# Attention scores of two heads side by side in the two row halves of TensorE, in three groups over two banks

## What is computed

```
B, S = 2, 512      # x is redrawn with this shape
H, KVH, HD = 32, 8, 64
q = apply_rope((xn @ Wq.T) as (b, H, s, HD))
k = apply_rope((xn @ Wk.T) as (b, KVH, s, HD));  v = (xn @ Wv.T) as (b, KVH, s, HD)
k, v repeated over the 4 heads of a group
logits = einsum('bhqd,bhkd->bhqk', q, k) * HD ** -0.5, masked causally
attn = softmax(logits);  out = einsum('bhqk,bhkd->bhqd', attn, v)
s = out.reshape(b, s, H * HD) @ Wo.T
```

## Time and profile before

| | |
|---|---|
| median of 3 runs | 783.19 us (781.56 to 783.24) |
| profiled execution: time, span | 780.78 us, 779.0 us |
| mean granted TensorE clock | 0.968 |
| PE (TensorE matmul) busy | 706.5 us, 91% |
| DVE (VectorE) busy | 477.7 us, 61% |
| ACT (ScalarE) busy | 417.9 us, 54% |
| POOL (GpSimd) busy | 399.3 us, 51% |

### The profile page before, as it was taken

One profiled execution on the slowest core, in us unless ns is written; L12 is line 12 of the kernel. 1 busy time (PEld: TensorE's weight loads), 2 busy tenths in 40 slices (PEclk: granted clock), 3 DMA queues, 4 the chain that ended last, 5 costly groups with the idle time before them and its releaser, 6 DMA issues.

```text
span 779.0 us, 13360 instructions
## 1 busy us (share of the span) xinstructions
PE 706.5 (91%) x4536; PEld 618.6 (79%) x4536; DVE 477.7 (61%) x1023; ACT 417.9 (54%) x1043; POOL 399.3 (51%) x451
## 2 busy tenths in 40 slices
PE   2999999999999991388889999999999999999995
PEld 2887989989989981266678888888888888888874
DVE  7582644423323445485566787777877778777764
ACT  4446244233233234236467776677766777667663
POOL 1412442332332220326777776787767877677460
PEclk9899999999999996599899999999999999999999
DMA  5075877778787505235224323322233222232001
GB/s 187 28 253 186 280 251 249 237 253 254 248 254 250 171 15 155 41 116 147 82 69 117 67 62 69 89 69 64 65 69 89 71 58 67 58 89 56 1 1 54
DMA packets 101859, 96.21 MB, mean 124 GB/s; under 512 B 50592, under 2 KB 72032, under 8 KB 101664
## 3 DMA queue, kind: packets, MB, share of 16 engines
q1 hardware_dynamic: 99584, 89.33, 39.6%
q0 software_dynamic: 2208, 6.03, 2.2%
HBM read 69.24 MB, written 9.31 MB: 101 GB/s over the span
## 4 chain that ended last, share of the span: by engine, by line
PE 64%; DVE 10%; POOL 9%; ACT 8%; issue 6%; SPq 1%; POOLq 1%; DMA 1%; DVEq 0%; ACTq 0%
PE bank L1631 15%; PE bank L1491 8%; PE bank L1665 8%; PE bank L1492 8%; PE bank L1493 8%; PE bank L1487 6%; POOL prob L1449 5%; ACT prob L1264 3%; PE bank L1752 3%; DVE nmax L1010 2%; PE bank L1753 2%; POOL q_lo L1461 2%; ACT kv_hi L1271 2%; DVE o_lo L1023 1%; POOL wq_lo L1429 1%
## 5 line engine op out<-in xcount | busy, mean ns | idle before, releaser
L1449 POOL TENSOR_TENSOR prob<-prob,rinv 128x128 f32<-128x128 f32 (+3 forms) x256 | 177.6, 724 | 102.1 <-DVE rinv L1015 102.1
L1264 ACT ACTIVATE prob<-bank,nmax 128x512 f32<-128x512 f32 (+3 forms) x256 | 133.2, 528 | 45.4 <-DVE nmax L1010 43.9
L1019 DVE TENSOR_TENSOR kv_lo<-bank,kv_hi 128x512 fp32r<-128x512 f32 x160 | 110.0, 687 | 52.7 <-ACT kv_hi L1271 51.8
L1271 ACT ACTIVATE kv_hi<-bank 128x512 fp32r<-128x512 f32 x160 | 96.3, 602 | 78.7 <-PE bank L1487 78.6
L1631 PEld LDWEIGHTS bank<-xgT,wm 128*128 128x128 f32 x920 | 108.1, 192 | 5.3 <-issue 3.8
L1631 PE MATMUL bank<-xgT,wm 128*128 128x128 f32 x920 | 110.3, 275 | 0.5 <-ACT xgT L1173 0.5
L1487 PE MATMUL bank<-cst,prob 128*128 128x128 f32 x640 | 97.8, 276 | 3.0 <-POOL prob L1449 1.2
L1010 DVE TENSOR_REDUCE nmax<-bank 128x1 f32<-128x512 f32 (+2 forms) x192 | 91.1, 502 | 10.8 <-PE bank L1755 10.2
L1491 PE MATMUL bank<-kv_hi,v_lo 128*128 128x128 f32 (+3 forms) x256 | 93.2, 364 | 0.3 <-DVE kv_lo L1019 0.3
L1752 PE MATMUL bank<-kT,qT 128*128 128x512 f32 (+3 forms) x256 | 81.6, 324 | 11.2 <-ACT prob L1264 7.2
L912 DVE TENSOR_TENSOR hE<-sil,bank 128x512 f32<-128x512 f32 x23 | 15.8, 688 | 111.0 <-PE bank L1631 80.5
(11 more groups left out here) (301 smaller groups left out, 1479.0 us busy)
## 6 DMA issues: line engine op xcount, KB each, us to landing
wm<-in_w_moe SPq DMA_DIRECT2D x23, 1280.0 KB
wm<-in_w_moe SPq DMA_DIRECT2D x23, 640.0 KB, 5.7
qT<-q_hi SPq DMA_DIRECT2D x124, 64.0 KB, 2.0
qT<-q_lo SPq DMA_DIRECT2D x124, 64.0 KB, 2.0
k_exp<-k_rows SPq DMA_DIRECT2D x56, 64.0 KB, 2.0
wtl<-in_w_moe_tail SPq DMA_DIRECT2D x46, 64.0 KB
gy<-y_rows SPq DMA_DIRECT2D x8, 256.0 KB, 4.8
wq_raw<-in_w_qkv SPq DMA_DIRECT2D x32, 64.0 KB, 2.5
```

What stands on the lines that cost most here:

```text
L1019: TT(p_lo[:, b_, :], bank[2 + b_ % 2][:, :], p_hi[:, b_, :].bitcast(F32), ALU.subtract).then_inc(plo_done, 1)
L1264: ins = actv(prob[:, i % 2, h, POFF[j]:POFF[j] + (j + 1) * P], bk[:, at:at + (j + 1) * P], ACT.Exp, bias=nmax[:, i % 2, h, j:j + 1], accum ...
L1271: actv(p_hi[:, b_, :], bank[2 + b_ % 2][:, :], ACT.Copy).then_inc(phi_done, 1)
L1449: ins = GT(seg, seg, rinv[:, i % 2, k, j:j + 1].to_broadcast([P, (j + 1) * P]), ALU.mult)
```

## The change

- `SCORES` has three groups per pair instead of five. A group holds the same blocks j for both heads: block 3; blocks 2 and 0; block 1. Head 0 goes to bank 0, head 1 to bank 1, so each group fills both banks.
- `qT` and `kT` keep their size; a head's high and low part of q now lie in two slots on the same 64 rows, head 0 on rows 0 to 63 and head 1 on rows 64 to 127. A score is the sum of three products over 64 rows (low q with high k, high q with low k, high with high); the product of the two low parts is left out. The products of the two heads alternate, placed at array row 0 and row 64.
- The mask is one product per head: 6 a pair instead of 5, 1024 columns instead of 1280.
- S and E stand at steps 0, 1.7 and 3.4 of a pair instead of 0 to 4; N of the two heads at 4.6 and 6 instead of 3 and 5.
- S waits until the exponential of the group just before it is done, and E for each head's maxima.
- One reciprocal serves both heads, and waits for all three groups of the pair. Maxima: 8 reductions per pair instead of 7.
- The DMAs that move q keep their number and size; only their target rows change.

```diff
-SCORES = [[(0, 3, 0)], [(0, 2, 0), (0, 0, 3 * P)], [(0, 1, 0), (1, 1, 2 * P)], [(1, 3, 0)], [(1, 2, 0), (1, 0, 3 * P)]]
...
-MASKS = [(3 * P, 3 * P), (2 * P, 2 * P), (P, 0), (3 * P, 3 * P), (2 * P, 2 * P)]
-HEADS_AT = (3, 5)
+SCORES = [[(3, 0)], [(2, 0), (0, 3 * P)], [(1, 0)]]
...
+MASKS = [(3 * P, 0, P), (2 * P, 2 * P, 2 * P), (P, 0, P)]
+SCORES_AT = (0, 1.7, 3.4)
+HEADS_AT = (4.6, 6)
...
+PARTS = 3 * PAIRS
...
-            own += [(n, 2, "S", r, k), (n, 4, "E", r, k), (n + LAG, 3, "T", r, k), (n + LAG + TO_V, 5, "A", r, k)]
+            own += [(n + LAG, 3, "T", r, k), (n + LAG + TO_V, 5, "A", r, k)]
+        for k in range(3):
+            own += [(5 * r + SCORES_AT[k], 2, "S", r, k), (5 * r + SCORES_AT[k], 4, "E", r, k)]
...
-                        sp.wait_ge(score_full, g * STEPS + (b * 10 + 10 - STEPS))
+                        sp.wait_ge(score_full, g * PARTS + (b * 6 + 6 - PARTS))
...
-                            sp.dma_start(qT[(at + i) * 32:(at + i + 1) * 32, b, h, :].bitcast(F32),
+                            to = (h % 2 * 2 + i) * 32
+                            sp.dma_start(qT[to:to + 32, b, h // 2 * 2 + at // 2, :].bitcast(F32),
...
-                        bk = bank[(i + k) % 2]
-                        dve.wait_ge(score_full, u + 1)
-                        segs = SCORES[k]
-                        if k == 2:
-                            vec.tensor_reduce(out=nmax[:, i % 2, :, 1:2], in_=bk[:, :].rearrange("p (h n) -> p h n", h=2),
-                                              op=ALU.max, axis=AX.X, negate=True).then_inc(max_ready, 1)
-                        else:
-                            for h, j, at in segs:
-                                ins = vec.tensor_reduce(out=nmax[:, i % 2, h, j:j + 1], in_=bk[:, at:at + (j + 1) * P],
+                        dve.wait_ge(score_full, q * 3 + (k + 1))
+                        for h in range(2):
+                            for j, at in SCORES[k]:
+                                ins = vec.tensor_reduce(out=nmax[:, i % 2, h, j:j + 1], in_=bank[h][:, at:at + (j + 1) * P],
...
-                        dve.wait_ge(exp_done, q * 5 + (HEADS_AT[k] + 2))
-                        vec.reciprocal(rinv[:, i % 2, k, :], rsum[:, i % 2, k, :]).then_inc(rinv_ready, 1)
+                        if k == 0:
+                            dve.wait_ge(exp_done, q * 3 + 4)
+                            vec.reciprocal(rinv[:, i % 2, :, :], rsum[:, i % 2, :, :]).then_inc(rinv_ready, 1)
...
-                    ins = TT(qT[(2 + i) * 32:(3 + i) * 32, 0, h, :], q_mix[hs, i, 0, :], q_hi[hs, i, :].bitcast(F32), ALU.subtract)
+                    ins = TT(qT[(2 * h + i) * 32:(2 * h + i + 1) * 32, 0, 1, :], q_mix[hs, i, 0, :], q_hi[hs, i, :].bitcast(F32), ALU.subtract)
...
-                    act.wait_ge(score_full, now * STEPS + (i * 10 - 10))
+                    act.wait_ge(score_full, now * PARTS + (i * 6 - 6))
...
-                        bk = bank[(i + k) % 2]
-                        act.wait_ge(max_ready, u + 1)
...
-                        for h, j, at in SCORES[k]:
-                            ins = actv(prob[:, i % 2, h, POFF[j]:POFF[j] + (j + 1) * P], bk[:, at:at + (j + 1) * P], ACT.Exp,
-                                       bias=nmax[:, i % 2, h, j:j + 1], accum_out=rsum[:, i % 2, h, j:j + 1])
+                        for h in range(2):
+                            act.wait_ge(max_ready, q * 6 + (2 * k + h + 1))
+                            for j, at in SCORES[k]:
+                                ins = actv(prob[:, i % 2, h, POFF[j]:POFF[j] + (j + 1) * P], bank[h][:, at:at + (j + 1) * P], ACT.Exp,
+                                           bias=nmax[:, i % 2, h, j:j + 1], accum_out=rsum[:, i % 2, h, j:j + 1])
...
-                    ins = actv(qT[i * 32:(i + 1) * 32, 0, h, :], q_mix[hs, i, 0, :], ACT.Copy)
+                    ins = actv(qT[(2 * h + i) * 32:(2 * h + i + 1) * 32, 0, 0, :], q_mix[hs, i, 0, :], ACT.Copy)
...
-            act.sem_inc(exp_done, 2)
+            act.sem_inc(exp_done, 1)
...
-                        gp_.wait_ge(rinv_ready, q * 2 + (k + 1))
+                        gp_.wait_ge(rinv_ready, q + 1)
...
-                        pe.wait_ge(exp_done, u + 1)
-                        for h, j, at in SCORES[k]:
-                            n = (j + 1) * P
-                            dst = bank[(i + k) % 2][:, at:at + n]
-                            qs = qT[:, b, 2 * (i % 2) + h, j * P:(j + 1) * P]
-                            mm(dst, qs, kT[:, b, 0, 0:n], start=(h, j, at) == SCORES[k][0], stop=False)
-                            mm(dst, qs, kT[:, b, 1, 0:n], start=False, stop=False)
-                        lo, moved = MASKS[k]
-                        mm(bank[(i + k) % 2][:, lo:HALF], mask_b[:, :], id_b[:, moved:moved + HALF - lo], start=False,
-                           stop=True).then_inc(score_full, 1)
+                        pe.wait_ge(exp_done, q * 3 + (k + 1))
+                        for q_part, k_part in ((1, 0), (0, 1), (0, 0)):
+                            for j, at in SCORES[k]:
+                                for h in range(2):
+                                    hs = slice(h * HD, (h + 1) * HD)
+                                    mm(bank[h][:, at:at + (j + 1) * P], qT[hs, b, i % 2 * 2 + q_part, j * P:(j + 1) * P],
+                                       kT[hs, b, k_part, 0:(j + 1) * P], start=q_part == 1 and at == 0, stop=False,
+                                       tile_position=(h * HD, 0))
+                        lo, moved, n = MASKS[k]
+                        for h in range(2):
+                            ins = mm(bank[h][:, lo:lo + n], mask_b[:, :], id_b[:, moved:moved + n], start=False, stop=True)
+                        ins.then_inc(score_full, 1)
...
-            pe.wait_ge(exp_done, KVH * STEPS + 2)
+            pe.wait_ge(exp_done, KVH * PARTS + 1)
...

```

## The result

The changed kernel takes 894.78 us (median of 4 runs, 894.52 to 899.74); the kernel before on the same chip 782.38 (781.16 to 783.24). The ratio is 1.1483, with a 95% interval of 1.1449 to 1.1516: slower by 14.8%. The prediction said 884, within 815 to 915. The profiled execution spans 892.8 us where it was 779.0, and the mean granted clock is 0.931 instead of 0.968.

What follows compares the result with a forecast made beforehand. TensorE alone was taken to bound the kernel before. 780.8 + 92 (middle g 73, last 13, first 6) + 9 for the clock = 882, 884 as a median; range 860 to 900, 8 in 10 for 815 to 915.

Steps and rivals of the forecast that it cites:

- Side and mechanism: Slower (0.92); TensorE's busy share falls from 99% to about 80%, idle ahead of transposes 3.3 us bare, 0.7 full.
- bare pair: Attention pair without W or Q products, where a full pair has two of each; 9.4 us before, 15.0 forecast.
- Columns: Score products on TensorE: 3.2 us a pair taken, between 2.4 and 4.4, against 3.3 before.
- rival 3: Array must run empty between full and half use: 0.34 us a pair, +11, so 895; chance 0.09.
- Banks: Each group waits for the last one's maxima and exponentials: S1 to next S0 8.2 us bare, 8.8 full.
- Reciprocal: Late reciprocal and scaling delay T to 4.1 us after S0 in a full pair, 5.3 bare, 0.5 more with w_o's copy.
- The clock: Lower clock behind 3.3 us idle in bare pairs: about 1.3 each, 18 over 14, half counted, 9 us.
- couple: One full and one bare pair together: 30.5 us forecast instead of 24.4, +73 over 12 in the six middle g.
- The ends: First and last g of the attention: +6 us in the first, +13 in the last.
- The banks alone: Scaled probabilities come in time, only the wait for the last group's exponentials is left: 820 us; chance 0.18.
- No side-by-side: Products of the two row halves do not overlap; S1 costs 0.4 more in 32 pairs: +12, 896 us; chance 0.09.
- TensorE still the bound: Waits fit beside other work if S1 to next S0 stays below some 5.5 us: 755 or 780 us; chance 0.08.

Runs made afterwards that it cites:

- e2: Changed kernel with the reciprocal for both heads moved earlier, from step 4.6 to 3.95: 839.72 us, 1.0782 of the kernel before.
- e6: Kernel before, with each score group waiting for the exponential of the group just before instead of two back: 864.64 us, 1.1074.
- e7: Kernel before, with one late reciprocal for both heads behind all five groups: 837.79 us, 1.0744.
- e5: Kernel before, with its 160 mask products over rows 0 to 63 only: 801.79 us, 1.0279.
- e1: Changed kernel with the 128-row products and q layout of the kernel before: 889.95 us, 1.1423 of the kernel before.
- e3: Changed kernel with 14 needless TensorE products per bare pair ahead of the wait for scaled probabilities: 877.84 us, 1.1255 of the kernel before.
- e9: Changed kernel with reciprocal at step 2.95, S2's maxima and exponentials earlier, and a rotation moved: 835.61 us, 1.0734 of the kernel before.
- e4: Changed kernel with all three products of head 0, then all of head 1, instead of alternating: 913.69 us, 1.1728 of the kernel before.

## Why the prediction was right, point by point

**Side and mechanism: right.** TensorE went from 99% to 83% busy in a g (predicted 80%), and the largest wait stands ahead of the T that needs the scaled probabilities: 3.56 us in a bare pair and 0.36 in a full one (predicted 3.3 and 0.7); in bare pairs without w_o's copy it is 3.04. The second is the wait for ScalarE's exponentials ahead of S2 and S0. GpSimd still waits for the reciprocal. e2, e6 and e7 show both causes by themselves. They don't add up: 58 and 84 alone, 112 together with the products. Each covers part of the other, since a group that starts late also gives the reciprocal time.

**Columns: the sum nearly right, by two errors that cancel.** At full clock the score groups of a pair take 1.02, 1.23 and some 0.67 until T starts, 2.92 in all; I took 3.2, between 2.4 and 4.4. The sum itself is sound (its 1.95 for S1 without side-by-side adds up to 1.92, and the masks of before have 1152 columns a pair, not 1280). The choice of 0.11 for each load was wrong. TensorE's loads ahead of S2, all six of them:

```profile
667.41 0.41 PEld L1753 LDWEIGHTS bank<-kT,qT 64*128 64x128 f32 x6 [0.97 <-ACT prob L1265]
```

Loads of 128 rows are 0.11 apart. Six of them, one behind the other, would take 5 x 0.11 and the last load's own 0.19, 0.74 together; three pairs take 2 x 0.11 + 0.19 = 0.41, as measured. So loads of the two halves lie side by side. The rule that I weighed (the Trainium skill, TensorE: Matmul & The Clock Gate, section LDWEIGHTS: a load costs by its columns and not its rows) says what one load costs. I had stretched it to a pair of loads in different halves, and here two of them cost no more than one. Against this stands what rival 3 named: the products of S0 need 0.70 (3 x 0.235) but the mask comes after 0.89, so 0.19 on leaving half use; and S1 starts 0.33 after a 512-column product (677.89 to 678.22) that holds the array 0.235, so 0.1 on entering. The rule in TensorEngine Tiling (Array Packing), section Tiling Modes, of the Trainium skill (a change of the tiling mode drains TensorE) is borne out by these rows and by e5. As a rival for the end time it falls, since the groups stay cheaper than before's 3.3 all the same, and e1, with none of it, has pairs of the same length wherever both are at full clock.

**Banks: right in the sum, in part by luck.** From S1 to the next S0 I had 8.2 in a bare pair and 8.8 in a full one; it is 8.56 (662.74 to 671.30) and 8.53 (678.22 to 686.75). The two exponentials of S1 take 1.81, as I had. But the maxima start 1.43 after S1 at full clock, where I had 1.73, and 1.90 in the bare pair, at the lower level. And between those exponentials and the maxima of S2 I had laid three high parts in a row on ScalarE and one low part on VectorE, 2.15 in a bare pair and 2.75 in a full one. It is 2.45 (667.24 to 669.69) and 2.98, and what fills it are three low parts, two of T and the output's between them. I had missed two of these. VectorE's timeline after:

```profile
667.88 0.69 DVE L1020 TENSOR_TENSOR kv_lo<-bank,kv_hi 128x512 fp32r<-128x512 f32 x1 [1.83 <-ACT kv_hi L1272]
668.49 0.68 DVE L1024 TENSOR_TENSOR o_lo<-bank,o_hi 128x512 fp32r<-128x512 f32 x1
669.09 0.68 DVE L1020 TENSOR_TENSOR kv_lo<-bank,kv_hi 128x512 fp32r<-128x512 f32 x1
```

**Reciprocal: right.** T at 5.8 after S0 in a bare pair with w_o's copy and 5.3 in one without; it is 5.87 (654.38 to 660.25) and 5.35 (686.75 to 692.10). In a full pair 4.1; it is 4.07.

**The clock: mis-sized, the step that failed most.** In all twelve bare pairs of the middle g T, A and S1 ran in part or whole at the lower level behind the wait. Measured against e3 at full clock, T and A take 1.09 more and S1 0.46 more in the pair shown, which is 1.56 longer (16.92 against 15.36). In the bare pairs without w_o's copy S1 is slow throughout (2.20) and the pair is 2.16 longer (17.00 against 14.84). I had priced this at 1.3 and then counted half, 9 us. 1.86 on average over 16 bare pairs is 30 (an estimate from these rows), and the products of e3, which kept most of the attention at 1.00, made it 18 us faster. Without the clock the sum of a couple was right to 0.1: at full clock, in e3, it takes 30.6 where I had 30.5. With the low clock it takes 32.4, so the six middle g cost 95.1 where 73 and the clock's 9 stood.

**The ends.** First g +3.9 (I had 6), last g with the tail +18.9 (13): a bare pair there takes 15.28, where I had 13.5, a full one 15.45, where I had 14.9, and what is left falls behind the last S0. The 4.0 us by which the attention starts earlier lie within what one execution differs from another (349.63 to 354.65 above); 2.5 of them are there before the first score already (below). So that the forecast of 884 lies only 1.2% under the 894.78 owes something to luck: the middle g cost 13 us more than I had, the ends 4 more, and 4 came back by the early start.

**The rivals.** "The banks alone" is nearly what e2 and e9 are: 840 and 836 where I had 820; it needed the reciprocal to come early, which the written order did not give. "No side-by-side" is out by S0's 0.90 and by e4. "TensorE still the bound" needed some 5.5 (its terms add up to 5.25) from S1 to the next S0 and got 8.5.

**Whether the form could ever win here** is not settled. Three groups that fill both banks make a chain of scores, maxima, two exponentials and handovers; e9 comes to 12.02 for a bare pair, in which TensorE has about 9 us of work, and it needs 24.4 for a couple to be level. That this chain is the limit is argued from e9's rows; no run here took it away, for instance with four banks for scores.

## What to carry to other kernels

Before packing two heads into the array, count the banks: if the packed group fills all the buffers of its stage, the next one can't start before the last is read, and that price (84 us alone) was many times what the cheaper groups saved (0.4 us a pair at full clock, 12 us in all). When a reduction is merged over two heads, look at what stands ahead of it in that engine's list, and at who waits behind it; here one number in the order was worth 55 us, the clock's share with it. An idle time of some 3 us on TensorE can cost more than itself: the work behind it ran at the lower clock in all twelve middle bare pairs of the changed kernel and in seven of twelve in e1.

## What was not expected of the hardware

- Weight loads over 64 rows in alternating halves lie two by two side by side: six take 0.41 us, where six at the 0.11 of 128-row loads would take 0.74.
- Going from full to half use of the array and back cost 0.136 to 0.153 us per group in e5, and 0.1 on entering and 0.19 on leaving in the changed kernel.
- Three products in a row on one half ahead of three on the other cost nothing against alternating them; six in a row cost 0.35 us (e4).
- 224 needless products made a kernel 18 us faster (e3).
- The clock's fall is not decided by the length of an idle time alone. Behind 3.39 us it stayed at 1.00 in e1 (above), behind 3.04 it fell in the changed kernel. Ahead of the attention the kernel before and the changed one have the same wait, 2.37 and 2.36 us; in the three microseconds from 1.4 us behind it on, the granted clock is 0.50 in the one and 1.00 in the other. A row of TensorE's timeline and a stretch (columns as in the earlier trace rows), before:

```profile
342.62 0.50 PE L1491 MATMUL bank<-xnT_hi,kv_lo 128*128 128x512 f32 x1 [2.37 <-DVE xnT_lo L972]
```

```profile
344.00:347.00 3.00, 3.00 (x9) 2.35 (x8) 1.87 (x3) 0.00 (x0) 0.00 (x0) 0.50 0.17 44
```

  and after:

```profile
340.13 0.50 PE L1492 MATMUL bank<-xnT_hi,kv_lo 128*128 128x512 f32 x1 [2.36 <-DVE xnT_lo L977]
```

```profile
341.50:344.50 3.00, 3.00 (x15) 2.41 (x14) 3.00 (x6) 0.00 (x0) 0.00 (x0) 1.00 0.17 44
```
